# A two-attention image kernel: the second attention's values copied on VectorE, and the engines' lists rewritten

## What is computed

```python
# first block: sparse attention on the low band, N = 1024, 8 heads of 16
attn = jnp.einsum('bhnd,bhmd->bhnm', l2norm(q), l2norm(k)) * scale
_, idx = jax.lax.top_k(attn, N // 2)        # the larger half of each row is kept
attn = softmax(where(kept, attn, -1e9)); out = attn @ v
# high bands: y = silu(gn(conv3x3 depthwise)); h + alpha * gn(conv1x1(y))
# join the bands; ffn: gn(w2 gelu(gn(w1 x))), added to x
# second block, N = 4096, width 16 for q and k
q, k, v = Wq x + bq, Wk x + bk, Wv x + bv
out = gamma * (Wo softmax(q k^T) v + bo) + x
```

## Time and profile before

| | |
|---|---|
| times of three runs | 5553.13, 5548.35, 5555.53 us |
| median | 5553.13 us |
| the profiled execution | 5553.66 us |
| its span | 5551.9 us |
| busy PE / DVE / ACT / POOL | 4778.7 / 4622.0 / 4261.9 / 261.5 us |

### The profile page before, as it was taken

One profiled execution on the slowest core, in us unless ns is written; L12 is line 12 of the kernel. 1 busy time (PEld: TensorE's weight loads), 2 busy tenths in 40 slices (PEclk: granted clock), 3 DMA queues, 4 the chain that ended last, 5 costly groups with the idle time before them and its releaser, 6 DMA issues.

```text
span 5551.9 us, 93420 instructions
## 1 busy us (share of the span) xinstructions
PE 4778.7 (86%) x30180; PEld 3098.8 (56%) x30180; DVE 4622.0 (83%) x9087; ACT 4261.9 (77%) x6779; POOL 261.5 (5%) x125
## 2 busy tenths in 40 slices
PE   4444899988999889988999889998899989997899
PEld 2000366654666456664666546665566636665588
DVE  4887789987999789987899879998799979996553
ACT  3884699948998599966999589984999769995333
POOL 2001000020000200010000100002000100000000
PEclk7555899998999989998999989999899989998899
DMA  1001200012001110012000120011200120001100
GB/s 58 8 10 52 62 15 16 13 60 64 16 21 44 38 53 18 16 61 63 15 16 13 60 64 16 17 47 35 55 16 18 55 69 15 16 13 44 35 12 16
DMA packets 103270, 185.34 MB, mean 33 GB/s; under 512 B 48536, under 2 KB 53560, under 8 KB 98008
## 3 DMA queue, kind: packets, MB, share of 16 engines
q1 hardware_dynamic: 102744, 178.93, 10.5%
HBM read 107.99 MB, written 67.37 MB: 32 GB/s over the span
## 4 chain that ended last, share of the span: by engine, by line
DVE 37%; PE 31%; issue 19%; ACT 7%; SPq 2%; DMA 1%; POOL 1%; DVEq 1%; ACTq 0%; POOLq 0%
PE PS L621 12%; DVE M L1798 8%; DVE MX L1966 7%; DVE work L1789 5%; PE PS L587 4%; PE PS L561 3%; ACT work L1216 3%; DVE work L1781 3%; DVE arena L1895 3%; PE PS L605 3%; PE PS L551 2%; PE PS L483 2%; ACT work L1271 1%; PE PS L1090 1%; PE PS L633 1%
## 5 line engine op out<-in xcount | busy, mean ns | idle before, releaser
L621 PEld LDWEIGHTS PS<-V,work 128*128 128x128 f32 x16384 | 2112.1, 193 | 164.6 <-ACT work L1281 23.1
L621 PE MATMUL PS<-V,work 128*128 128x129 f32 x16384 | 2130.1, 277 | 13.7 <-ACT work L1281 12.4
L1216 ACT ACTIVATE work<-arena,T 128x1024 bf16<-128x1024 f32 x1504 | 1714.9, 1145 | 23.4 <-DVE T L1709 13.1
L1966 DVE TENSOR_REDUCE MX<-PS 128x1 f32<-128x512 f32 x2048 | 1394.9, 686 | 249.9 <-PE PS L587 235.4
L1281 ACT ACTIVATE work<-PS 128x1024 f32<-128x1024 f32 x1024 | 1041.6, 1019 | 319.1 <-PE PS L605 317.2
L587 PE MATMUL PS<-KP,QP 96*128 96x512 bf16 x2048 | 844.0, 413 | 71.7 <-DVE MX L1966 32.8
L1798 DVE MAX8 M<-work 128x8 f32<-128x512 f32 x1024 | 651.2, 680 | 0.5
L605 PE MATMUL PS<-QP,KP 99*128 99x512 bf16 x2048 | 624.0, 387 | 23.2 <-ACT work L1281 19.8
L1208 ACT ACTIVATE arena<-PS 128x1024 f32<-128x1024 f32 x512 | 524.0, 1023 | 147.0 <-PE PS L483 138.5
L1895 DVE SCALAR_TENSOR_TENSOR arena<-PS,work 128x512 f32<-128x512 f32 x896 | 600.9, 683 | 33.7 <-ACT work L1271 24.3
L1271 ACT ACTIVATE work<-PS 128x512 f32<-128x512 f32 x896 | 513.8, 591 | 116.0 <-PE PS L551 112.8
(11 more groups left out here) (193 smaller groups left out, 4157.7 us busy)
## 6 DMA issues: line engine op xcount, KB each, us to landing
work<-scr SPq DMA_DIRECT2D x752, 32.0 KB, 1.8
work<-in_x SPq DMA_DIRECT2D x16, 1024.0 KB, 7.4
arena<-in_x SPq DMA_DIRECT2D x8, 2048.0 KB, 11.2
scrX<-arena SPq DMA_DIRECT2D x8, 2048.0 KB, 6.4
XR<-scrX SPq DMA_DIRECT2D x64, 256.0 KB, 2.7
out<-YO SPq DMA_DIRECT2D x64, 256.0 KB, 2.0
scr<-work SPq DMA_DIRECT2D x24, 512.0 KB, 2.7
scrL<-work SPq DMA_DIRECT2D x24, 512.0 KB, 7.9
```

The lines of the kernel that those rows point to most:

```text
L621: last = mm(PS[:, 5 + i // 2, 136 * (i % 2):136 * (i % 2) + 129], P1[:, (16 * j + k) % 3, t, 128 * i:128 * i + 128], V1[:, mt, :], start=( ...
L1216: A(junk[:, m % 2, :], scores(h, i), ACT.Sign, scale=-1.0, bias=T[:, h % 2, i:i + 1], accum_out=CA[:, h % 2, i:i + 1]).then_inc(s["ca"], 1)
L1966: V.reduce_max(MX[:, c % 2, i, w:w + 1], PS[:, maxbank(c, k, l0), :], AX.X).then_inc(s["mr"], 1)
```

## The change

Two things are changed. The copies of `values1` move from ACT to DVE, where they become `tensor_copy` (L2393 of the changed code); the semaphores, the tiles and the banks are the same. And the lists of PE, ACT and DVE are written in another order: in `between` above all, but also in `search`, `closing`, `alone` and the loop around `search`. The lists of SP and POOL are as before.

```diff
@@ ACT, between @@
-                def values1(k):
-                    if not fin:
-                        return
-                    act.wait_ge(s["v1p"], f * 8 + k + 1)
-                    A(V1[:, 4 * k:4 * k + 4, 0:128], PS[:, 2 + k % 2, :].rearrange("p (m c) -> p m c", c=128), ACT.Copy)\
-                        .then_inc(s["v1c"], 1)
@@ DVE, between @@
+                def values1(k):
+                    if not fin:
+                        return
+                    dve.wait_ge(s["v1p"], f * 8 + k + 1)
+                    V.tensor_copy(V1[:, 4 * k:4 * k + 4, 0:128], PS[:, 2 + k % 2, :].rearrange("p (m c) -> p m c", c=128))\
+                        .then_inc(s["v1c"], 1)
@@ PE, list of between, from points(1, 0) @@
                 points(1, 0)
+                group(4)
                 points(1, 1)
-                group(4)
                 ungroup(4)
                 points(2, 0)
                 points(2, 1)
+                score0(0)
                 qk1()
-                score0(0)
+                score0(1)
+                group(2)
                 values1(0)
-                score0(1)
                 values1(1)
                 score0(2)
                 values1(2)
+                values1(3)
...
@@ DVE, list of between, its end @@
                 points(2, 1)
+                moments(2)
                 part1(1)
+                variance(2)
+                values1(0)
+                values1(1)
+                values1(2)
                 centre0(0)
-                moments(2)
                 part1(2)
-                variance(2)
+                values1(3)
+                scales(2)
+                values1(4)
+                values1(5)
+                values1(6)
+                values1(7)
                 centre0(1)
-                scales(2)
@@ DVE, list of search @@
                     flip(h, 2)
+                    flip(h, 3)
                     maxima(h + 1, 0)
-                    flip(h, 3)
...
@@ PE, loop around search @@
                     if h < NH: weigh(h - 1, 4)
+                    if h < NH: weigh(h - 1, 5)
                     l1_turn(h - 1)
-                    if h < NH: weigh(h - 1, 5)
                     score(h + 1, 1)
                     if h < NH: weigh(h - 1, 6)
-                    if h >= 0: maxima(h + 1, 0)
                     l1_score(h, 0)
                     if h < NH: weigh(h - 1, 7)
+                    if h >= 0: maxima(h + 1, 0)
```

More of the change, by code:

```diff
@@ L727, in search @@
                     half_t(h - 1, 0, 0)
+                    maxima(h, 18)
+                    l1_score(h - 1, 10)
                     half_t(h - 1, 0, 1)
-                    maxima(h, 18)
                     l1_weigh(h - 1, 9, (0,))
@@ L1150, in between @@
                 ffn2(3)
+                spread(3)
+                group(1)
                 ffn2(4)
-                group(1)
+                ungroup(1)
                 ffn2(5)
-                ungroup(1)
-                spread(3)
                 ffn2(6)
```

469 lines of the change are left out of this document (229 added, 240 removed).

## The result

| kernel | median us (lowest to highest) | ratio to before (95%) |
|---|---|---|
| before | 5553.33 (5548.35 to 5563.05), 13 runs | |
| changed | 5543.22 (5538.03 to 5546.05), 13 runs | 0.998 (0.9971 to 0.9988) |

What follows compares the result with a forecast made beforehand. No single engine bounds it: PE, VectorE and ScalarE are within 7% of full in the search, and a chain bounds the part between images. 5553.7 - 3 - 14 - 9 = 5527.7, forecast 5528, range 5503 to 5560.

Steps and rivals of the forecast that it cites:

- Item 1: Between images: eight copies per image on VectorE, 5.5 us, fall within 11.1 us of waits and cost 0.
- Item 2: Between images: first maxima start earlier, 1.5 us in each of two images, 3 in all, bounds 0 and 6.
- Item 3: Between images: the chain to part1 gets shorter by 2.0 us per image, 14 us over 7 images.
- (a): Between images: group(4) first lets POOL start earlier, so 0.85 of PE's 1.40 us wait before ungroup(4) goes.
- (b): Between images: ScalarE's evict0(0) and points evictions come ahead of qk1, taking 1.0 us off the chain.
- (c): Between images: ScalarE's copy between part1(0) and part1(1) goes, gaining 0.15 us.
- Item 4: Closing of an image: 1.1 us of half_e waits covered plus 0.2 from mix(2), 1.3 per image, 9 us.
- the lock's inheritance: Closing: with mix(2) early, POOL's chain catches the next two-input operation, so only 0.2 of 2.6 us is won.
- Item 5: Search, 42 heads: reordering gives -0.4 to +0.2 us per head, taken as 0, with 17 us either side.
- The rival: Search loses: l1_turn behind weigh, maxima behind l1_score, 0.9 us per head, +38 over 42 heads; 5568, chance 0.14.
- Item 6: Opening and the end stretch with one attention alone: the same kinds of permutation, 0, 3 us either side.
- The rival by SP: Between images: score0(0) ahead of qk1 needs SP's loads, qk1 0.7 us later, only closing's 9 remains; 5545, chance 0.24.

Runs made afterwards that it cites:

- E2: The kernel before with only the changed part between images (copies on VectorE and the lists there): 5522.89 us, ratio 0.995.
- E7: E2 plus all changed lists of the search (PE, ACT and DVE), with closing and opening as before: 5546.17 us, ratio 0.9992.
- E5: The changed kernel with the closing's lists (PE, ACT and DVE) as before: 5551.20 us, ratio 0.9998.
- E3: The kernel before with only the values' copies moved to VectorE, all other calls in their old order: 5544.09 us, ratio 0.9986.
- E4: The changed kernel with the values' copies back on ScalarE, other calls in the changed order: 5552.31 us, ratio 1.0002.
- E14: E2 plus the changed closing lists on PE, ACT and DVE: 5532.53 us, ratio 0.9965.
- E12: E2 with only l1_turn moved behind one more weigh at the head's start on PE: 5520.81 us, ratio 0.9941.
- E6: E2 with PE's changed head start, l1_turn behind one more weigh and first maxima behind l1_score and the last weigh: 5562.61 us, ratio 1.0023.
- E11: E2 with only the first maxima moved behind l1_score and the last weigh at the head's start on PE: 5568.12 us, ratio 1.0028.
- E15: E2 plus the changed lists of image 0's lone first attention and the places of DVE's update calls in first: 5526.97 us, ratio 0.9956.

## Why the prediction was right or wrong

Predicted 5528.0, measured 5543.22. The order in which the parts are added matters; along one path, by medians: the part between images -29.4 (E2), the search +23.3 (E7), the opening +5.0 (E5), the closing -8.0 (the changed kernel), together -9.1, against -10.1 directly.

- **Item 1, the copies (0).** Right in its price: 691 ns against 687 taken. They are not quite off the path: in four parts of E3 PE's first maximum waits for the last copy, 3.5 us in all, but it waited 5.7 in seven for ScalarE's, and the wait for scrL behind it covers more than that.
- **Item 2, the start of the maxima (3).** Right in its mechanism, too small in size. The start comes earlier and ends in the wait for scrL, 22.9 us in E3 and 10.1 in the changed kernel where 2.7 was. But the whole was worth 8.2 (E3) and 9.1 (E4): in the two parts with the long dip 4.4 and 4.8 came in where I took 1.5 each, half of what stood open, and a third part with a shorter dip was overlooked. The clock behind the maxima, which moves along, was not in the sum at all.
- **Item 3, the chain to part1 (14).** Right in sum, wrong in place. (a) 1.40 of waiting for POOL fell away, and norm 2 stands 1.67 nearer to the last product. (b) and (c) gave 0.86, but points(1,1), moved in between the norms, took 0.48 of it; counted from norm 2 part1 is 0.4 earlier and not 2.0. That is 2.06 an image, 14.4 in seven. E2 has another 6 to 7 us ahead of the last product, but that is the stretch whose time goes with the clock. So the part between images won 29 us and not 17, and the missing 12 are mostly item 2's.
- **Item 4, the closing (9).** 8.0 in the kernel that was forecast (E5), so right in size. The threshold's delay was forecast (1.6, measured 1.35), and the lock's inheritance too (7.8 to 8.1). What was missing is the last head, which PE and VectorE take from two different lists: it adds 0.85 an image to the gain beside the changed search and takes 0.95 from it beside the old one, where the closing costs 9.6 (E14). That the gain lies behind the threshold, with VectorE as the bound, fits E5 (10.3) and not the profiles of E2 and E14 (nothing); it stays open, and with it how far the 8.0 was luck.
- **Item 5, the search (0).** This is the step that failed. The walk through the lists gave -0.4 to +0.2; it is +0.30 in the middle heads and +0.88 in the last, and with what the first image has on top 19.7 us for the 42 heads; beside the old closing the last head has 1.72, and the search costs 23.3. The rival named the place (first maxima behind l1_score, l1_turn behind weigh) and had 0.9: 0.56 for the turn, which is nothing (E12), and 0.34 for the maxima with VectorE's flip(3) ahead of them. PE's start of the head alone is 0.80 (E6). I let the 1.43 that PE waits for the threshold take it up. E11 shows that wait unchanged while the period grows by the full delay: it is the end of VectorE's own chain, which runs from the first maximum to the threshold. What the other changed lists do to bring 0.80 down to 0.30 was not taken apart.
- **Item 6 (0).** 4 to 5 lost in the opening (E15; E5 against E7).
- **The rival by SP** is refuted: PE's score0(0) stands ahead of qk1 with no wait (L483 at 1281.31).

Along that path the gains of items 2 and 3 were taken 12 too small, the closing's 1 too large, the opening's loss was left out (5) and the search was 23 worse than taken. The first error hid half of the last; that the time is no further off than 15 is luck.

## What to carry to other kernels

Of a list that is written anew, ask stage by stage how often it runs: 0.3 us in a loop of 42 outweighs 1.5 us in a part that comes seven times. A wait on one engine for the result of another's chain is no slack for work that the chain itself waits for; follow the chain from its first instruction. And try each stage's list by itself, but judge it beside the lists it will run with, since lists of several engines are cut to each other: the same closing costs 9.6 us beside one search and wins 8.0 beside the other. A profile is one execution; set it against the median of its kernel before a difference of some us is given to a list. Here the change without two thirds of its edits is three times as good.

## What the runs showed of the hardware

The granted clock during the values' products fell to 0.50 for 14 us in two, for 7 and 3.4 us in two more of seven parts between images that run the same instructions, and not in the other three; with eight copies of 0.6 us moved from ScalarE to VectorE it was gone from there (E3). Behind the first maxima it stood at 0.50 for 37.5 us in most parts and for up to 44.4, again with the same instructions. The time by which VectorE's operations with two inputs in SBUF exceed their 1.22 us beside POOL's sums to 7.8, 8.1 and 6.7 us an image for three orders of the same operations: it depends little on which of them overlap POOL's operations.
